# A cross-attention and quantized feed-forward kernel on one core: weight pieces turned as two-byte numbers, and the orders of all engines written anew

## The chip, the cores and the metric

The kernel runs on one core of a Trainium2 chip, in one launch. The metric is the device time of an execution in microseconds (us), as the median of the runs shown. TensorE multiplies and transposes into PSUM, VectorE (DVE), ScalarE (ACT) and GpSimd (POOL) work on tiles, and SyncE (SP) issues nearly all transfers.

## The reference

Eight items of 512 tokens with 512 features attend to 120 context rows with 16 heads, then pass a feed-forward layer whose weights are quantized to -1, 0 and 1 and whose activations are rounded to 8-bit steps:

```
x = x + attention(layernorm(x), ctx, ctx, mask, wq, bq, wk, bk, wv, bv, wo, bo)   # softmax over 120 keys
scale = 1 / clip(mean(|w|), 1e-5)
wq = clip(round(w * scale), -1, 1) / scale            # for w1 [2048, 512] and w2 [512, 2048]
xq = round(rmsnorm(x) * s) / s, s = 127 / max|row|
h = gelu(xq(layernorm(x)) @ wq1.T + b1)
x = x + xq(h) @ wq2.T + b2
```

## The kernel before, in words

The tokens are 32 tiles of 128 (four to an item). Attention goes by units n = 0 to 127, four to a tile (four heads each); normalize(n), exps(n) and turn_probs(n) belong to unit n. ffn_up(k, c) makes one of four chunks of the hidden row of tile k, ffn_down(k, half) the output. Each engine has one queue, written out by hand as a list of calls in order; four passes of a loop (a = 2 to 5) hold the middle, and lists without a loop the start and the end. An engine does its list strictly in order, and semaphores hold it where it needs another's result.

The weights w1 and w2 come in eight pieces of 128 x 2048 (piece 0 to 3 of w1, 4 to 7 of w2). Each is summed in absolute value on ScalarE or VectorE (sum_abs), TensorE adds up the sums (total_weights(0) after w1's four, total_weights(1) after w2's), and weight_scales gives w_inv. GpSimd rounds the piece in place (round_piece, two passes), TensorE turns it in 16 blocks of 128 x 128, four to a bank, alternately into ps_z and ps_y (turn_piece(j, quarters), j the place in TURN), and evac_piece copies each bank as fp8 into w1T or w2T, ps_z by ScalarE and ps_y by VectorE. A bank can't be written again before it is copied. The rounding adds MAGIC = 12582912 so that float32 itself rounds; the second pass clips, and the copy subtracts MAGIC:

```
gp.tensor_scalar(piece, piece, w_inv[:, m:m + 1], MAGIC, ALU.mult, ALU.add)
gp.tensor_scalar(piece, piece, MAGIC + 1.0, MAGIC - 1.0, ALU.min, ALU.max)
```

The attention weights are split into a high and a low part for products of three passes; for wo, ScalarE makes the high part (round_wo) and VectorE the low one (split_wo), from a stage that wq used before. The loads of pieces 5, 6 and 7 wait for buffers to come free. Where tile k's rounded rows q_x or q_h are wanted turned, SyncE issues a transposing transfer (turn_x, turn_h). keep_busy runs turns of the identity whose results nobody reads.

Of the kernel before, what the change touches and what calls it, by code (L numbers as in the profile page):

```python
# [28 lines left out]
def xattn_bitffn_kernel(nc, x, ctx_in, mask, wq, bq, wk, bk, wv, bv, wo, bo, w1, b1, w2, b2, out):  # L29
# [105 lines left out]
    with ExitStack() as stack:  # L135
# [17 lines left out]
        ident = sb("ident", [P, P])  # L153
        neg_half = sb("neg_half", [P, T])
# [164 lines left out]
        def _(sp):  # L319
# [62 lines left out]

            for t in range(T):
                sp.dma_start(xn[:, t], xt_v[0, t]).then_inc(s[f"first{t}_in"], 16)
# [8 lines left out]
            sp.wait_ge(s["turn_full"], YT_N[("x", 0, 3)] + 1)  # L393
            sp.dma_start(xn[:], x_v[1]).then_inc(s["x_in"], 16)
            sp.wait_ge(s["turn_full"], YT_N[("k", 0, 0)] + 1)
            sp.dma_start(ctx_s, ctx_in[1]).then_inc(s["ctx_in"], 16)
            sp.wait_ge(s["wq_split"], 1)
            sp.dma_start(stage.rearrange("p (k n) -> p k n", k=KD), wo.rearrange("(k p) n -> p k n", p=P)
                         ).then_inc(s["wo_in"], 16)
            sp.dma_start(bv_row[:], bv.rearrange("(a d) -> a d", a=1).to_broadcast([S2, D])).then_inc(s["bv_in"], 16)  # L400
            load_piece(4)
            for v, dst in ((bo, bo_row), (b1, b1_row), (b2, b2_row)):
                sp.dma_start(dst[:], v.rearrange("(a d) -> a d", a=1).to_broadcast([P, v.shape[0]])
                             ).then_inc(s["bias_in"], 16)

            load_residual(0)
            load_piece(6)
            load_piece(5)
            load_piece(7)
            load_x(2)  # L410
            load_residual(3)
            load_mask(1)
            load_residual(1)
            load_residual(2)
            turn_x(0)
            load_residual(5)
            load_ctx(2)
            turn_x(1)
            turn_x(2)
            load_residual(4)  # L420
            load_x(3)
            turn_h(0)
            turn_x(3)
            turn_h(1)
            store(0)
            load_mask(2)
            load_ctx(3)
            turn_h(2)
            store(1)
            load_residual(6)  # L430
            load_residual(7)
            turn_x(4)
            turn_h(3)

            for a in range(2, 6):
# [3 lines left out]
                store(4 * a - 5)  # L439
                turn_x(4 * a - 2)  # L440
                turn_h(4 * a - 4)
                load_x(a + 2)
                load_residual(4 * a + 1)
                turn_h(4 * a - 3)
                turn_x(4 * a - 1)
                store(4 * a - 4)
                load_mask(a + 1)
                load_ctx(a + 2)
                store(4 * a - 3)
                load_residual(4 * a + 3)  # L450
                load_residual(4 * a + 2)
                turn_x(4 * a)
                turn_h(4 * a - 2)
                turn_h(4 * a - 1)

            turn_x(21)
            turn_x(22)
            store(18)
            turn_h(20)
            load_residual(24)  # L460
            store(19)
            turn_x(23)
            turn_h(21)
            load_residual(25)
            load_mask(7)
            store(20)
            load_residual(26)
            turn_x(24)
            store(21)
            turn_h(22)  # L470
            turn_x(25)
            load_residual(27)
            turn_h(23)
            turn_x(26)
            store(22)
            turn_h(24)
            store(23)
            load_residual(28)
            turn_x(27)
            load_residual(29)  # L480
# [7 lines left out]
            load_residual(31)  # L488
            turn_h(27)
            turn_x(30)  # L490
            turn_h(28)
            turn_x(31)
            store(26)
            turn_h(29)
            turn_h(30)
            turn_last(0)
# [10 lines left out]
        def _(pe):  # L507
# [205 lines left out]
            def first_q(w, m, i):  # L713
# [3 lines left out]
                return last  # L717
# [1812 lines left out]
```

## Time and profile before

| | us |
|---|---|
| median of 3 runs | 658.78 |
| lowest, highest | 658.63, 660.31 |
| the profiled execution | 659.41 |
| its span in the profile | 657.6 |
| TensorE busy | 633.0 |
| VectorE busy | 576.8 |
| ScalarE busy | 528.3 |
| GpSimd busy | 517.9 |

The span runs from the first to the last instruction, the time of an execution includes what lies around it. Busy time counts instructions that overlap once. Matmuls are pipelined: their durations are longer than the distance from one to the next, which is read from the chain or from starts.

### The profile page before, as it was taken

To read this page: it belongs to the slowest core of one execution; us is meant where nothing else is said; L and a number is where in the kernel's file an instruction comes from. 1 tells how busy PE (TensorE), PEld (TensorE's weight loads), DVE (VectorE), ACT (ScalarE), POOL (GpSimd) and SP (SyncE) were. 2 spreads that over 40 slices of the span, in tenths; PEclk is the share of its full clock that TensorE was granted. 3 is DMA by queue.
4 is the path that set the end of the run, shared out by engine and by line. 5 is a ranking of instruction groups with operands and counts; after the bars stand their busy time and mean duration, and the time that the engine had idled before them with its cause. 6 is when DMAs were issued, how large, how long until landed. Compare 5 with 4: busy or idle time off the path is not lost.

```text
span 657.6 us, 14093 instructions
## 1 busy us (share of the span) xinstructions
PE 633.0 (96%) x4896; PEld 425.3 (65%) x4896; DVE 576.8 (88%) x1062; ACT 528.3 (80%) x1450; POOL 517.9 (79%) x653
## 2 busy tenths in 40 slices
PE   7969999999999999999999999999999999999996
PEld 6646786566666766666666666666766666666542
DVE  6578789999998989999899989999889898999994
ACT  2459678888888688888988788897989979999764
POOL 3276898679986898768877798768976788989875
PEclk9979999999999999999999999999999999999999
DMA  8991320225135324144344334243322323234336
GB/s 288 380 334 66 95 74 9 78 52 125 42 74 137 72 73 89 41 114 103 73 73 109 76 97 57 72 114 88 87 41 61 74 84 57 58 89 100 79 77 164
DMA packets 109285, 65.38 MB, mean 99 GB/s; under 512 B 90855, under 2 KB 90855, under 8 KB 108575
## 3 DMA queue, kind: packets, MB, share of 16 engines
q1 hardware_dynamic: 108159, 64.49, 37.1%
q8 instruction: 39, 0.64, 0.4%
q14 instruction: 31, 0.25, 0.1%
q10 hardware_dynamic: 1056, 0.00, 0.1%
HBM read 35.12 MB, written 8.39 MB: 66 GB/s over the span
## 4 chain that ended last, share of the span: by engine, by line
PE 60%; POOL 17%; DVE 7%; DMA 6%; ACT 5%; issue 4%; SPq 1%; POOLq 0%; DVEq 0%; ACTq 0%
PE ps_a L545 21%; PE ps_z L659 10%; PE ps_y L682 10%; PE ps_t L618 6%; PE ps_s L608 3%; POOL hid L2223 3%; POOL prob L2212 3%; PE ps_a L630 3%; POOL q_h L2228 3%; DMA x<-in_L_xattn_wo_dram 2%; PE ps_y L552 1%; PE ps_a L579 1%; POOL x L2207 1%; POOL x L2175 1%; PE ps_s L682 1%
## 5 line engine op out<-in xcount | busy, mean ns | idle before, releaser
L1110 ACT ACTIVATE prob<-ps_s,nmax 128x120 f32<-128x120 f32 x512 | 179.5, 381 | 17.3 <-PE ps_t L618 8.6
L2212 POOL TENSOR_TENSOR prob<-prob,pinv 128x480 f32<-128x480 f32 x128 | 128.9, 1011 | 60.9 <-DVE pinv L1545 60.3
L659 PE MATMUL ps_z<-w1T,q_xT 128*128 128x512 fp8e4 x476 | 122.6, 380 | 0.8 <-DVE hid L1586 0.5
L1110 ACT ACTIVATION_READ_ACCUMULATOR prob<-ps_s,nmax 128x1 f32 x512 | 115.7, 226 | 0.0
L682 PE MATMUL ps_y<-w2T,q_hT 128*128 128x512 fp8e4 x448 | 105.0, 379 | 1.3 <-DMA q_hT<-q_h 1.2
L1586 DVE SCALAR_TENSOR_TENSOR hid<-ps_z,y_deq,b_row 128x512 f32<-128x512 f32 x119 | 87.9, 739 | 11.2 <-PE ps_z L659 9.1
L1537 DVE COPY_PREDICATED_SCALAR ps_s<-hidden_key,masked_c 128x480 f32 x128 | 90.4, 706 | 0.7 <-PE ps_s L608 0.6
L1088 ACT COPY probT<-ps_t 120x512 f32<-120x512 f32 x128 | 76.8, 600 | 16.9 <-PE ps_t L618 14.5
L1540 DVE TENSOR_REDUCE nmax<-ps_s 128x4 f32<-128x480 f32 x128 | 84.2, 657 | 4.4
L618 PE MATMUL ps_t<-ident,prob 128*120 128x128 f32 x512 | 78.0, 275 | 2.2 <-ACT probT L1088 1.3
L618 PEld LDWEIGHTS ps_t<-ident,prob 128*120 128x120 f32 x512 | 60.2, 137 | 26.4 <-ACT probT L1088 5.2
L682 PEld LDWEIGHTS ps_y<-w2T,q_hT 128*128 128x128 bf16 x448 | 42.5, 98 | 50.3 <-issue 5.6
L659 PEld LDWEIGHTS ps_z<-w1T,q_xT 128*128 128x128 bf16 x476 | 42.8, 98 | 45.9 <-issue 8.7
L1594 DVE TENSOR_REDUCE hs<-hid 128x1 f32<-128x2048 f32 x31 | 70.4, 2271 | 0.9 <-ACT hid L1117 0.4
L2223 POOL TENSOR_SCALAR hid<-hid,hs 128x2048 f32<-128x2048 f32 x31 | 61.2, 1975 | 7.4 <-ACT q_h L1151 3.7
L1117 ACT ACTIVATE hid<-hid 128x2048 f32<-128x2048 f32 x31 | 59.3, 1914 | 3.9 <-DVE hid L1586 3.6
L2228 POOL TENSOR_SCALAR q_h<-hid 128x2048 bf16<-128x2048 f32 x28 | 53.8, 1920 | 2.5
L545 PE MATMUL ps_a<-wo_h,oT_h 128*128 128x512 f32 x128 | 54.2, 424 | 0.0
L1151 ACT ACTIVATE q_h<-hid 128x2048 bf16<-128x2048 f32 x28 | 54.2, 1934 | 0.0
L545 PE MATMUL ps_a<-wo_h,oT_l 128*128 128x512 f32 x128 | 50.4, 394 | 0.0
L545 PE MATMUL ps_a<-wo_l,oT_h 128*128 128x512 f32 x128 | 50.0, 391 | 0.0
L545 PE MATMUL ps_a<-xnT_h,wq_h 128*128 128x512 f32 x112 | 47.3, 422 | 0.0
(207 smaller groups left out, 1382.9 us busy)
## 6 DMA issues: line engine op xcount, KB each, us to landing
x<-in_x_dram SPq DMA_DIRECT2D x32, 256.0 KB, 3.0
out_dram<-x SPq DMA_DIRECT2D x32, 256.0 KB, 2.4
xn<-in_x_dram SPq DMA_DIRECT2D x7, 1024.0 KB, 6.2
hid<-in_L_ffn_w_dram SPq DMA_DIRECT2D x4, 1024.0 KB, 8.9
ctx_k<-in_ctx_dram SPq DMA_DIRECT2D x8, 240.0 KB, 3.1
ctx_k<-in_mask_Bx1xSxS_ik_dram SPq DMA_DIRECT2D x7, 240.0 KB, 3.1
xn<-in_x_dram SPq DMA_DIRECT2D x4, 256.0 KB, 4.8
x<-in_L_xattn_wq_dram SPq DMA_DIRECT2D x1, 1024.0 KB, 8.4
```

The lines of the kernel that those rows point to most:

```text
L545: last = nc.tensor.matmul(bank, w, m, start=(k == 0 and i == 0), stop=(k == KD - 1 and i == 2))
L618: last = nc.tensor.transpose(ps_t[0:S2, g * P:(g + 1) * P], prob[:, n % 3, g * S2:(g + 1) * S2], ident[:])
L659: last = nc.tensor.matmul(bank[:], q_xT[:, k % 3, i], w1T[:, i, c * CH:(c + 1) * CH], start=(i == 0), stop=(i == KD - 1))
L682: last = nc.tensor.matmul(y_bank(k)[:], turned_h(k)[:, f], w2T[:, f], start=(f == 0), stop=(f == KF - 1))
L1088: nc.scalar.copy(probT[0:S2, i], ps_t[0:S2, :].rearrange("p (g q) -> p g q", g=G)).then_inc(s["p_evac"], 1)
L1110: last = nc.scalar.activation(prob[:, n % 3, g * S2:(g + 1) * S2], ps_s[n % HG][:, g * S2:(g + 1) * S2], ACT.Exp, bias=nmax[:, n % 4, g:g ...
L1537: v.copy_predicated(sc, hidden_key[:, k // T % 2, k % T].unsqueeze(1).to_broadcast([P, G, S2]), masked_c[:].unsqueeze(2).to_broadcast([P, ...
L1540: v.tensor_reduce(out=nmax[:, n % 4], in_=sc, op=ALU.max, axis=AX_X, negate=True).then_inc(s["sc_max"], 1)
L1586: v.scalar_tensor_tensor(hidden(k)[:, c * CH:(c + 1) * CH], z_bank(FC * k + c)[:], y_deq[:, k % 8:k % 8 + 1], b1_row[:, c * CH:(c + 1) * C ...
L2212: gp.tensor_tensor(pr, pr, pinv[:, n % 4].unsqueeze(2).to_broadcast([P, HG, S2]), ALU.mult).then_inc(s["prob_ready"], 1)
L2223: gp.tensor_scalar(magic(k), hidden(k), hs[:, 5, t:t + 1], MAGIC, ALU.mult, ALU.add).then_inc(s["h_magic"], 1)
L2228: gp.tensor_scalar(rounded(k), hidden(k), 1.0, -MAGIC, ALU.mult, ALU.add).then_inc(s["qh_ready"], 1)
```

## The change

It has three parts. First, the second pass of round_piece takes MAGIC off, clips above at 1 and writes two-byte numbers (bfloat16) into the low half of the piece's own buffer; TensorE turns these with a two-byte identity into two-byte views of the banks; the copies clip below, ScalarE by the sign, VectorE by a maximum with -1. Second, first steps are moved: on SyncE the loads of wv, wo, bv, the biases and the second context, on TensorE the first project_ctx and 20 idle turns for 12, on VectorE hide, split_wq and weight_scales. Some waits go with them (wk_in is waited for in project_ctx, the bias columns in evac_q and add_bk). Third, the lists of all engines have a new order throughout, in the loop too, with the same calls in them.

```diff
+        ident_b = sb("ident_b", [P, P], BF16)
+        turned_z, turned_y = ps_z[:].bitcast(BF16)[:, 0:CH], ps_y[:].bitcast(BF16)[:, 0:CH]
+        def low_half(p):
+            return piece_buf[p].bitcast(BF16)[:, 0:F]
...
-            for p in range(4):
-                load_piece(p)
-            sp.dma_start(wv_s[:], wv.rearrange("(k p) n -> p k n", p=P)).then_inc(s["wv_in"], 16)
...
+            load_piece(0)
+            load_piece(2)
+            load_bv()
+            load_piece(1)
+            load_piece(3)
+            load_x(1)
+            load_wo()
+            load_wv()
+            load_next_ctx()
             load_piece(4)
...
             def turn_piece(j, quarters):
                 p = TURN[j]
+                if j == 0:
+                    pe.wait_ge(s["consts_pool"], 5)
...
-                        last = nc.tensor.transpose(bank[:, c * P:(c + 1) * P], piece_buf[p][:, col:col + P], ident[:])
+                        last = nc.tensor.transpose(bank[:, c * P:(c + 1) * P], low_half(p)[:, col:col + P], ident_b[:])
...
-                nc.scalar.activation(dst, src, ACT.Copy, bias=-MAGIC, saturate=False).then_inc(s["wT_act"], 1)
+                nc.scalar.activation(dst, src, ACT.Sign, saturate=False).then_inc(s["wT_act"], 1)
...
-                v.tensor_scalar(dst, src, -MAGIC, None, ALU.add, saturate=False).then_inc(s["wT_dve"], 1)
+                v.tensor_scalar(dst, src, -1.0, None, ALU.max, saturate=False).then_inc(s["wT_dve"], 1)
...
-                gp.tensor_scalar(piece, piece, MAGIC + 1.0, MAGIC - 1.0, ALU.min, ALU.max
+                gp.tensor_scalar(low_half(p), piece, -MAGIC, 1.0, ALU.add, ALU.min
                                  ).then_inc(s["w_ready_pool"], 1)
...
+            gp.tensor_copy(ident_b[:], ident[:]).then_inc(s["consts_pool"], 1)
...
             normalize(9)
+            round_piece(4)
+            ln1_factors(2, 0, 4, 9)
+            normalize(10)
             round_x(0)
```

GpSimd, behind its copy of wq's high part: L2263 and L2266 are the two passes of round_piece, L2157 to L2162 the factors of item 1's layernorm, L2168 its application to a tile, L2212 normalize. Before:

```order
L2263 TENSOR_SCALAR hid<-hid,w_inv 128x2048
L2266 TENSOR_SCALAR hid<-hid 128x2048
L2263 TENSOR_SCALAR hid<-hid,w_inv 128x2048
L2266 TENSOR_SCALAR hid<-hid 128x2048
L2157 TENSOR_SCALAR ln<-mv 128x4
L2160 TENSOR_TENSOR ln<-ln,neg_half 128x4
L2162 TENSOR_SCALAR ln<-mv 128x4
L2263 TENSOR_SCALAR raw_wk_h<-raw_wk_h,w_inv 128x2048
L2266 TENSOR_SCALAR raw_wk_h<-raw_wk_h 128x2048
L2212 TENSOR_TENSOR prob<-prob,pinv 128x480 x2
L2168 TENSOR_SCALAR xn<-xn,ln 128x512 x4
```

The same place in the change, where the lines are L2305, L2308, L2199 to L2204, L2210 and L2254:

```order
L2305 TENSOR_SCALAR hid<-hid,w_inv 128x2048
L2308 TENSOR_SCALAR hid<-hid 128x2048
L2199 TENSOR_SCALAR ln<-mv 128x4
L2202 TENSOR_TENSOR ln<-ln,neg_half 128x4
L2204 TENSOR_SCALAR ln<-mv 128x4
L2210 TENSOR_SCALAR xn<-xn,ln 128x512 x2
L2305 TENSOR_SCALAR hid<-hid,w_inv 128x2048
L2308 TENSOR_SCALAR hid<-hid 128x2048
L2305 TENSOR_SCALAR raw_wk_h<-raw_wk_h,w_inv 128x2048
L2308 TENSOR_SCALAR raw_wk_h<-raw_wk_h 128x2048
L2254 TENSOR_TENSOR prob<-prob,pinv 128x480 x3
L2210 TENSOR_SCALAR xn<-xn,ln 128x512 x2
```

The factors and two tiles of x moved ahead of pieces 1 and 2.

GpSimd again, from piece 6 or 7 to the first round_x (L2180 and L2185; q_hT is piece 4's buffer). Before:

```order
L2263 TENSOR_SCALAR hid<-hid,w_inv 128x2048
L2266 TENSOR_SCALAR hid<-hid 128x2048
L2212 TENSOR_TENSOR prob<-prob,pinv 128x480
L2180 TENSOR_SCALAR yw<-yw,yq 128x512
L2185 TENSOR_SCALAR q_x<-yw 128x512
L2212 TENSOR_TENSOR prob<-prob,pinv 128x480
L2263 TENSOR_SCALAR q_hT<-q_hT,w_inv 128x2048
L2266 TENSOR_SCALAR q_hT<-q_hT 128x2048
```

In the change, where round_x is L2222 and L2227:

```order
L2305 TENSOR_SCALAR hid<-hid,w_inv 128x2048
L2308 TENSOR_SCALAR hid<-hid 128x2048
L2254 TENSOR_TENSOR prob<-prob,pinv 128x480
L2305 TENSOR_SCALAR q_hT<-q_hT,w_inv 128x2048
L2308 TENSOR_SCALAR q_hT<-q_hT 128x2048
L2199 TENSOR_SCALAR ln<-mv 128x4
L2202 TENSOR_TENSOR ln<-ln,neg_half 128x4
L2204 TENSOR_SCALAR ln<-mv 128x4
L2254 TENSOR_TENSOR prob<-prob,pinv 128x480
L2222 TENSOR_SCALAR yw<-yw,yq 128x512
L2227 TENSOR_SCALAR q_x<-yw 128x512
```

The first round_x moved behind piece 4 and the factors of item 2.

TensorE at the end of a pass of the loop: L682 is ffn_down (x16 is both halves), L659 ffn_up, L618 turn_probs, L630 attend, L608 scores. Before:

```order
L618 MATMUL ps_t<-ident,prob 120x128 x4
L659 MATMUL ps_z<-w1T,q_xT 128x512 x4
L630 MATMUL ps_a<-probT,v_s 32x128 x16
L682 MATMUL ps_y<-w2T,q_hT 128x512 x16
L659 MATMUL ps_z<-w1T,q_xT 128x512 x4
L608 MATMUL ps_s<-keyT,qT 128x120 x16
```

In the change, in the same order of names L640, L681, L652, L704, L681, L630:

```order
L704 MATMUL ps_y<-w2T,q_hT 128x512 x8
L681 MATMUL ps_z<-w1T,q_xT 128x512 x4
L640 MATMUL ps_t<-ident,prob 120x128 x4
L652 MATMUL ps_a<-probT,v_s 32x128 x16
L704 MATMUL ps_y<-w2T,q_hT 128x512 x8
L681 MATMUL ps_z<-w1T,q_xT 128x512 x4
L630 MATMUL ps_s<-keyT,qT 128x120 x16
```

The first half of ffn_down moved ahead of one ffn_up, a turn_probs and attend.

## Rows read from the trace of the kernel before

**Rows 1.** The page: busy time by engine, the transfer rate by slice, one costly group.
```profile
PE 633.0 (96%) x4896; PEld 425.3 (65%) x4896; DVE 576.8 (88%) x1062; ACT 528.3 (80%) x1450; POOL 517.9 (79%) x653
...
GB/s 288 380 334 66 95 74 9 78 52 125 42 74 137 72 73 89 41 114 103 73 73 109 76 97 57 72 114 88 87 41 61 74 84 57 58 89 100 79 77 164
...
L2228 POOL TENSOR_SCALAR q_h<-hid 128x2048 bf16<-128x2048 f32 x28 | 53.8, 1920 | 2.5
```

**Rows 2.** Stretches: busy us of PE, PEld, DVE, ACT, POOL; clock, DMA share, GB/s.
```profile
33.00:50.00 17.00, 11.45 (x48) 7.19 (x48) 12.17 (x19) 8.53 (x30) 13.37 (x10) 0.80 0.91 320
...
62.00:98.00 36.00, 35.64 (x311) 28.38 (x312) 28.82 (x63) 26.49 (x104) 29.17 (x25) 1.00 0.26 77
98.00:160.00 62.00, 60.25 (x504) 39.51 (x503) 59.30 (x111) 54.00 (x154) 49.10 (x61) 1.00 0.23 58
160.00:550.00 390.00, 387.14 (x3044) 263.83 (x3036) 352.61 (x656) 330.51 (x923) 317.80 (x411) 1.00 0.34 81
```

**Rows 3.** The chain that ended last: start, length, what; x counts loads too.
```profile
22.54 13.77 DMA x<-in_L_xattn_wo_dram
...
40.80 5.26 PE ps_a L579 x8
...
62.96 3.43 PE ps_a L579 x8
...
82.57 0.44 PE ps_z L705 x4
...
83.88 1.05 PE ps_a L630 x32
...
98.03 0.86 PE ps_z L659 x4
...
252.60 3.56 PE ps_y L682 x16
...
639.12 4.24 DMA q_hT<-xn
```

**Rows 4.** Timeline of TensorE; the idle time before and its releaser stand in brackets.
```profile
38.86 1.09 PE L705 MATMUL ps_z<-ident,hid 128*128 128x128 f32 x4 [4.77 <-ACT w1T L1169]
...
61.91 0.36 PE L691 MATMUL ps_z<-w_abs,q_xT 128*128 128x4 f32 x2
...
97.86 1.03 PE L659 MATMUL ps_z<-w1T,q_xT 128*128 128x512 fp8e4 x4
```

**Rows 5.** VectorE's copies of turned pieces, by form, up to 140 us: busy us, mean ns.
```profile
L1672 DVE TENSOR_SCALAR w1T<-ps_y 128x512 fp8e4<-128x512 f32 x8 | 5.5, 688 | 5.6 <-PE ps_y L705 5.6
```

**Rows 6.** VectorE by form in the last 28 us.
```profile
L1632 DVE TENSOR_SCALAR probT<-qT 128x1024 bf16<-128x1024 f32 x1 | 0.7, 694 | 0.0
```

**Rows 7.** Timeline of GpSimd.
```profile
28.99 1.98 POOL L2263 TENSOR_SCALAR hid<-hid,w_inv 128x2048 f32<-128x2048 f32 x1 [15.33 <-DVE w_deq L1644]
...
37.37 1.02 POOL L2160 TENSOR_TENSOR ln<-ln,neg_half 128x4 f32<-128x4 f32 x1
...
49.66 3.02 POOL L2168 TENSOR_SCALAR xn<-xn,ln 128x512 f32<-128x512 f32 x4
...
65.68 2.88 POOL L2212 TENSOR_TENSOR prob<-prob,pinv 128x480 f32<-128x480 f32 x3 [5.83 <-DVE pinv L1545]
...
79.43 0.99 POOL L2212 TENSOR_TENSOR prob<-prob,pinv 128x480 f32<-128x480 f32 x1 [1.80 <-DVE pinv L1545]
...
85.68 0.69 POOL L2180 TENSOR_SCALAR yw<-yw,yq 128x512 f32<-128x512 f32 x1
```

**Rows 8.** Timeline of VectorE: the first statistics of item 1.
```profile
32.04 0.69 DVE L1523 BATCH_NORM_STATS2 bn<-xn 128x6 f32<-128x512 f32 x1 [3.16 <-DMA xn<-in_x_dram]
```

**Rows 9.** DMA issues, us to landing: turn_x, then turn_h.
```profile
q_xT<-q_x SPq DMA_TRANSPOSE x32, 2.4
q_hT<-q_h SPq DMA_TRANSPOSE x29, 4.3
```

**Rows 10.** Timeline of SyncE: the issue of ffn_down(6)'s turned rows, and the next.
```profile
246.17 12.82 SPq L352 DMA_TRANSPOSE q_hT<-q_h  x2
```

More of the change, by code:

```diff
@@ L938, in _ @@
             ffn_up(21, 1)
+            attend(23)
             ffn_down(19, 1)
-            attend(23)
+            ffn_up(21, 2)
             scores(25)
-            ffn_up(21, 2)
             turn_probs(97)
@@ L1054, in _ @@
             ffn_up(30, 2)
+            ffn_up(30, 3)
             ffn_down(27, 0)
-            ffn_up(30, 3)
             ffn_down(27, 1)
-            ffn_down(28, 0)
             ffn_up(31, 0)
@@ L1062, in _ @@
             ffn_up(31, 3)
+            ffn_down(28, 0)
             ffn_down(28, 1)
@@ L1809, in _ @@
+            invert_sums(19)
             softmax_max(20)
-            evac_up(1, 1)
-            invert_sums(19)
-            oT_low(3)
+            softmax_max(21)
             xT_low(2, 2)
-            softmax_max(21)
+            softmax_max(22)
             evac_up(1, 2)
-            softmax_max(22)
+            residual(3)
             invert_sums(20)
-            residual(3)
             softmax_max(23)
+            ln2_stats(3)
             evac_up(1, 3)
+            ln2_scales(3)
+            add_bv(2)
@@ L1907, in _ @@
                 residual(4 * a - 1)
+                evac_up(4 * a - 2, 0)
+                invert_sums(16 * a + 5)
                 softmax_max(16 * a + 7)
@@ L1964, in _ @@
             oT_low(22)
+            invert_sums(94)
             softmax_max(96)
+            invert_sums(95)
             xT_low(7, 0)
-            invert_sums(95)
+            evac_up(20, 3)
             softmax_max(97)
+            softmax_max(98)
+            residual(22)
+            evac_up(21, 0)
             invert_sums(96)
-            evac_up(20, 3)
-            residual(22)
+            ln2_stats(22)
             xT_low(7, 1)
-            softmax_max(98)
-            ln2_stats(22)
+            invert_sums(97)
@@ L2012, in _ @@
+            add_bk(7)
+            evac_up(23, 0)
             softmax_max(107)
-            invert_sums(104)
-            add_bk(7)
-            ln2_stats(24)
-            evac_up(23, 0)
             h_scale(22)
-            invert_sums(105)
             invert_sums(106)
-            ln2_scales(24)
-            invert_sums(107)
             evac_up(23, 1)
-            evac_down(21)
             oT_low(25)
             softmax_max(108)
+            softmax_max(109)
             evac_up(23, 2)
-            softmax_max(109)
@@ L2028, in _ @@
-            invert_sums(108)
             softmax_max(110)
             softmax_max(111)
+            evac_up(23, 3)
+            evac_down(21)
+            invert_sums(107)
+            hide(7, mask_in)
+            invert_sums(108)
+            residual(25)
+            ln2_stats(25)
             invert_sums(109)
-            evac_up(23, 3)
-            residual(25)
-            hide(7, mask_in)
-            ln2_stats(25)
+            ln2_scales(25)
             evac_up(24, 0)
-            ln2_scales(25)
+            invert_sums(110)
```

958 lines of the change are left out of this document (489 added, 469 removed).

## Prediction

> **What bounds the kernel now.** I read the page's shares first: TensorE is busy 633.0 of 657.6 us, VectorE 88%, ScalarE 80%, GpSimd 79% [rows 1]. An average over stages says little, so the stretches come next: from 160 to 550 us TensorE is busy 387.14 of 390 us, so no order of the same work can win more than 2.9 us there. Between 33 and 50 us it is busy 11.45 of 17 at a mean clock of 0.80, and from there to 98 us it is nearly full [rows 2]. The gain, if any, lies ahead of 98 us: in the 5.55 us that TensorE idles at 33 to 50, and in the work it does there.
>
> The chain says what holds it: the load of wo, issued at 22.54, lands 13.77 us later at 36.31 [rows 3]; ScalarE rounds wo ahead of its first copy of a weight piece, and TensorE waits 4.77 us for that copy's bank, until 38.86 [rows 4]. In the stretch behind this wait the granted clock is lower: eight passes over wv take 5.26 us at 40.80, and the like take 3.43 at 62.96 [rows 3]. The marks that I follow are the second total of the weights on TensorE (61.91) and the first ffn_up (97.86) [rows 4]: 35.95 us apart, TensorE nearly gapless between them [rows 2].
>
> **The cheaper transposes.** Four turns of two-pass float32 follow in 0.44 us, 110 ns each [rows 3]. A two-byte turn streams 128 columns in one pass. The nearest row is the 512-column product of one-pass operands, four in 0.86 us, 215 ns each [rows 3]; a quarter is 54. So 56 ns less each, 128 turns: 7.2 us of TensorE work. Bounds: 54 ns, and no gain (110). I take 54, since the passes over wv (429 ns for 512 columns, 3.43/8) show the same factor of two for float32 against one pass. On the path lie those between the two marks, 64 turns (pieces 4 to 7): 3.6 us. The other 64 lie where TensorE waits, and the wait hides them.
> The Trainium skill, TensorE: Matmul & The Clock Gate, section Back-to-back issue gap, speaks against a quarter: it gives about 81 ns for a sustained pair of a weight load and a 128-column product. By it, the 64 turns would save 1.9 us, TensorE's leg below would be 33.6 and pass GpSimd's, and the time would be 1.1 us above mine. No row of before shows such a pair in two-byte form.
>
> **The copies out of PSUM.** VectorE's now reads two-byte numbers and takes a maximum; it took 688 ns from float32 to fp8 [rows 5]. Not shown by any row. Above: 0.69 us, nothing won. Below: the two-byte output of 1024 elements from SBUF took 694 ns [rows 6], so 512 might take 0.35, 16 copies 5.4 us of VectorE, which would take away the loss of 1.8 below: 649.3. I take 0.69: source is PSUM and output one byte, as in the present row. ScalarE's Sign for Copy I leave at nothing: the order of the changed kernel has no table load among them. It has one pair of table loads more in the body, in ScalarE, which idles a fifth of the span [rows 1].
> The Trainium skill, DVE: opcode table, section Perf-mode slots, says that a one-source operation with an fp8 stream does not reach the modes that ask for two-byte source and destination. The sum by it is the sum above.
> GpSimd's second pass over a piece now writes two bytes: 1920 ns for such an output [rows 1] against 1.98 us for the first pass [rows 7]; a piece stays at 3.97 with the hand-over. The copy of the identity, 128 by 128, lies before GpSimd's factors, which wait for x anyway.
>
> **The moved loads.** wv goes behind x of item 1 and wo; bv goes ahead of them, and the second context behind. At 380 GB/s [rows 1] the megabyte is 2.8 us, bv's 0.24 MB 0.6. Piece 3 lands 0.6 later, so w_inv, for which GpSimd waited 15.3 us until 28.99 [rows 7], comes at 29.6. x lands at 32.04 - 2.8 + 0.6 = 29.8 [rows 8]; wo at 36.3 - 2.8 = 33.5 (bv's and the context's bytes cancel). wv lands last, about where wo did (36.3), still ahead of its use. SyncE then waits for the turned keys before piece 4 and the biases, until about 28.5. Their users come after 50 us, so nothing. On TensorE the first project_ctx goes ahead of first_q and eight more idle products stand ahead of x; both lie in front of w_inv, which is set by the loads: nothing, cover 1.5 to 2 us; without it as much would be paid.
>
> **To the first mark.** GpSimd's queue is now: piece 0, factors of item 1, two tiles of x, pieces 1 and 2, three normalizations, two tiles, piece 3, one normalization. Pieces 4 x 3.97 = 15.9; factors 1.7 (1.02 for the power, the rest two small ones and hand-overs); four tiles 3.0; four normalizations at 0.96 = 3.8 (2.88 for three) [rows 7]: 24.4 with nothing between. VectorE has its statistics of x ready at 29.8 + 4.1 = 33.9 (four of 0.69 [rows 8] with an aggregation each, and add_bk), 0.3 after piece 0. So 29.6 + 24.4 + 0.3 = 54.3, and with the turn and the total behind it 54.9. Before, the mark was 61.91. The other bound is ScalarE: from wo's landing to the mark were 25.6 us, which with wo at 33.5 gives 59.1 if no wait in it shortens. But ScalarE is busy 8.53 of 17 us at 33 to 50 [rows 2]; 3.3 of the idle lie ahead of wo, so some 5 of the 25.6 were waits for TensorE's turns, and its leg could end at 54. So I choose near the shorter: 55.9, 6.0 earlier.
>
> **To the first ffn_up.** GpSimd again: from the mark to piece 5's start 6.6 us as before (61.91 to 68.56) [rows 4, 7]; four pieces 15.9, normalizations 7 to 10 3.8, factors 1.7, round_x 1.4 (0.69 and about as much) [rows 7], the turn of q_x 2.4 [rows 9], 0.7 for the wait of normalization 8: 32.5, so 88.4. TensorE's own leg is 35.95 - 3.6 - 0.4 (one turn of probabilities moved behind) = 31.9, less than 32.5: GpSimd sets it by 0.6, since round_x(0) now stands behind piece 4 and the factors. 97.86 becomes 88.4: 9.5 earlier.
>
> **Behind it.** At 98 to 160 VectorE is busy 59.3 of 62 [rows 2]. Between evac_up(0, 0) and (0, 1) it now has ln2_scales(1) and a piece's copy where one softmax_max stood. It can keep the gain only as far as it was early itself. The loss is between nothing and the 3.5 us won between the marks; I take half, 1.8. The body (2.9 us of idle in 390) I take as unchanged. So is the end: TensorE there waits for the turn of q_h, 4.24 us from 639.12 [rows 3], behind GpSimd's round_h, and the square that now goes ahead of round_h(29) on ScalarE fits the wait.
> Sum: 9.5 - 1.8 = 7.7 us. The profiled execution took 659.41 (span 657.6 and 1.8 around it) and becomes 651.7; the median of the runs is 658.78, 0.6 less: **651.1**.
>
> **Rivals.** *A, the same path with another end* (0.58): 647 to 654.
> *B, GpSimd's queue holds the first ffn_up* (0.13). Normalization 8 started at 79.43, after a wait [rows 7], 17.5 after the mark, because its reciprocal stood behind residual(0). If it stays there: 55.9 + 17.5 = 73.4, then 1.0, pieces 6, 7, 4 11.9, two normalizations 1.9, factors 1.7, round_x 1.4, turn 2.4: 93.7, only 4.2 early; less 1.8 that is 656.4. For it: three things that wait for piece 4 now. Against: the reciprocal is ahead of residual(0) in the new order.
> *C, VectorE gives back all that was won between the marks* (0.08): 6.0 early, 652.8; or the turns cost what they did (0.02): TensorE's leg is 35.5, 3.0 over GpSimd's, 654.1.
> *D, the body and the end also gain* (0.06): 2.9 us of idle and half of the 4.24: up to 5 us, 646.
> *E, within 0.3%* (0.08): B, and the ScalarE bound of 59.1 too. The mark is then 2.8 early and the rest gives back: about 657.
> *F, slower* (0.05): ffn_down(4a - 2, 0) has moved ahead of an ffn_up, a turn and attend, 0.86 + 0.44 + 1.05 = 2.35 us earlier [rows 3]. Its q_hT was issued at 246.17 [rows 10] and lands 4.3 later [rows 9], at 250.5, used at 252.60 [rows 3]: 2.1 us of room. round_h stands one normalization (0.96) earlier, so 0.7 is left. If round_h comes 3.1 us late, because the reductions ahead of it on VectorE do, each of four passes of the loop loses 2.4, 9.6 in all, against 7.7 won: 660.7. It decides from about 2.7 us late on.
>
> **The numbers.** 651.1, range 646 to 656.5: D's lower end is left out in part, and E and F above; the lost share is about 0.17. 0.3% is 2 us, about what this kernel's runs can tell. Faster (A to D) 0.87, same (E) 0.08, slower (F) 0.05.
>
> **What would show it.** Right: turns four in 0.22 us; VectorE's piece copy at 0.69; TensorE's wait for the first copy's bank under 3 us; second total near 56; first ffn_up near 88, with TensorE waiting for q_xT; TensorE still idle under 4 us from 160 to 550. Wrong: turns at 0.32 or more for four, piece 3 ready after 57, DVE at full share from 85 on while TensorE idles, waits for q_hT in the loop.

## The result and the profile after

The changed kernel took 695.62 us (median of 4 runs, 694.57 to 695.95), the kernel before 659.07 beside it (658.63 to 660.31): a ratio of 1.056, 95% interval 1.054 to 1.058. I had forecast 651.1, faster. The profiled execution took 695.95, its span is 694.1.

First the shares on the page of after, which answer to [rows 1]: GpSimd has 40.1 us more work, no other engine over 7.3 more, and TensorE's share fell from 96% to 92%.

```profile
PE 640.3 (92%) x4904; PEld 430.4 (62%) x4904; DVE 579.8 (84%) x1062; ACT 533.0 (77%) x1452; POOL 558.0 (80%) x654
```

The stretches of after, with the columns of [rows 2], say where: the body at 160 to 550 us is as full as before, and nearly everything is lost ahead of it. There GpSimd is the busiest engine in every stretch, and from 50 us on TensorE's granted clock, which was 1.00 before, is down too.

```profile
33.00:50.00 17.00, 8.53 (x62) 5.41 (x60) 8.80 (x14) 7.18 (x21) 16.56 (x8) 0.80 0.47 158
50.00:62.00 12.00, 2.45 (x20) 1.84 (x21) 4.12 (x6) 4.34 (x12) 11.91 (x4) 0.56 0.75 272
62.00:98.00 36.00, 26.89 (x212) 18.61 (x210) 22.64 (x44) 21.12 (x69) 28.55 (x16) 0.83 0.17 56
98.00:160.00 62.00, 50.24 (x424) 37.02 (x423) 44.85 (x81) 38.45 (x124) 55.05 (x44) 0.88 0.08 22
160.00:550.00 390.00, 387.09 (x3050) 261.71 (x3049) 355.12 (x663) 335.94 (x926) 319.92 (x408) 1.00 0.36 83
```

TensorE's timeline of after names what it waits for (in brackets at a line's end), one of GpSimd's second passes (L2308) in each line with a wait but the last. The second total, 61.91 in [rows 4], now stands at 78.24, and the first ffn_up, 97.86 before, at 133.73.

```profile
40.15 0.58 PE L729 MATMUL ps_z<-ident_b,hid 128*128 128x128 bf16 x4 [6.82 <-POOL hid L2308]
...
61.62 0.61 PE L729 MATMUL ps_z<-ident_b,raw_wk_h 128*128 128x128 bf16 x4 [6.70 <-POOL raw_wk_h L2308]
...
78.24 0.42 PE L713 MATMUL ps_z<-w_abs,q_xT 128*128 128x4 f32 x2
...
116.83 0.61 PE L729 MATMUL ps_z<-ident_b,hid 128*128 128x128 bf16 x4 [6.50 <-POOL hid L2308]
...
133.73 1.02 PE L681 MATMUL ps_z<-w1T,q_xT 128*128 128x512 fp8e4 x4 [1.02 <-DMA q_xT<-q_x]
```

The eight waits for that line come to 36.4 us, in the list of waits of after by buffer:

```profile
PE ps_z L729 <- POOL hid L2308: 18.0, 4, 6.8
PE ps_z L729 <- POOL raw_wk_h L2308: 6.7, 1, 6.7
PE ps_z L729 <- POOL x L2308: 4.3, 1, 4.3
PE ps_z L729 <- POOL raw_wv_h L2308: 4.2, 1, 4.2
PE ps_z L729 <- POOL q_hT L2308: 3.2, 1, 3.2
```

GpSimd's groups by form give the reason (last columns: busy us, mean ns of one). The second pass takes 7.09 us, and the first pass over the same elements (L2305) 1.98, as in [rows 7]. The pass that writes two-byte q_h with (mult, add), on which I had rested my price [rows 1], is still at 1.91.

```profile
L2270 POOL TENSOR_SCALAR q_h<-hid 128x2048 bf16<-128x2048 f32 x28 | 53.5, 1909 | 2.5
...
L2308 POOL TENSOR_SCALAR hid<-hid 128x2048 bf16<-128x2048 f32 x4 | 28.4, 7092 | 0.3
...
L2305 POOL TENSOR_SCALAR hid<-hid,w_inv 128x2048 f32<-128x2048 f32 x4 | 7.9, 1979 | 17.4 <-DVE w_deq L1678 17.4
```

Three things set the new pass apart from the quick ones: its pair of operations (add, min), its place (the low half of its own source), and a clip with a two-byte output. The experiments begin there.

### The profile page after: what moved, and what is told of

The parts are those of the page before. It is cut to its first block, busy times and chain, and to the rows that moved or that the text cites. A ratio compares the mean times of both kernels' runs of the same rounds, so it can differ in the third digit from the quotient of the medians.

```text
span 694.1 us, 14117 instructions
## 1 busy us (share of the span) xinstructions
PE 640.3 (92%) x4904; PEld 430.4 (62%) x4904; DVE 579.8 (84%) x1062; ACT 533.0 (77%) x1452; POOL 558.0 (80%) x654
## 4 chain that ended last, share of the span: by engine, by line
PE 52%; POOL 29%; DVE 7%; issue 5%; DMA 3%; ACT 3%; SPq 0%; POOLq 0%; DVEq 0%; ACTq 0%
PE ps_a L567 16%; PE ps_z L681 9%; PE ps_y L704 9%; PE ps_t L640 5%; POOL prob L2254 5%; POOL hid L2308 4%; POOL hid L2265 3%; PE ps_s L630 3%; PE ps_a L652 3%; POOL q_h L2270 2%; DMA q_hT<-q_h 2%; PE ps_y L574 1%; DVE ps_s L1571 1%; POOL x L2249 1%; ACT prob L1141 1%
## 5 line engine op out<-in xcount | busy, mean ns | idle before, releaser
L2254 POOL TENSOR_TENSOR prob<-prob,pinv 128x480 f32<-128x480 f32 x128 | 129.2, 1013 | 37.0 <-DVE pinv L1579 36.8
L681 PE MATMUL ps_z<-w1T,q_xT 128*128 128x512 fp8e4 x476 | 123.5, 382 | 2.0 <-DMA q_xT<-q_x 1.5
L1141 ACT ACTIVATION_READ_ACCUMULATOR prob<-ps_s,nmax 128x1 f32 x512 | 111.8, 218 | 0.0
L704 PE MATMUL ps_y<-w2T,q_hT 128*128 128x512 fp8e4 x448 | 105.6, 379 | 1.3 <-DMA q_hT<-q_h 1.3
L640 PE MATMUL ps_t<-ident,prob 128*120 128x128 f32 x512 | 80.2, 280 | 2.3 <-POOL prob L2254 2.0
L640 PEld LDWEIGHTS ps_t<-ident,prob 128*120 128x120 f32 x512 | 60.6, 140 | 24.0 <-issue 6.8
L704 PEld LDWEIGHTS ps_y<-w2T,q_hT 128*128 128x128 bf16 x448 | 42.3, 98 | 50.8 <-issue 6.1
L681 PEld LDWEIGHTS ps_z<-w1T,q_xT 128*128 128x128 bf16 x476 | 43.0, 98 | 48.5 <-issue 9.0
L567 PE MATMUL ps_a<-wo_h,oT_h 128*128 128x512 f32 x128 | 56.3, 440 | 0.0
```

What stands on the lines that cost most here:

```text
L567: last = nc.tensor.matmul(bank, w, m, start=(k == 0 and i == 0), stop=(k == KD - 1 and i == 2))
L640: last = nc.tensor.transpose(ps_t[0:S2, g * P:(g + 1) * P], prob[:, n % 3, g * S2:(g + 1) * S2], ident[:])
L681: last = nc.tensor.matmul(bank[:], q_xT[:, k % 3, i], w1T[:, i, c * CH:(c + 1) * CH], start=(i == 0), stop=(i == KD - 1))
L704: last = nc.tensor.matmul(y_bank(k)[:], turned_h(k)[:, f], w2T[:, f], start=(f == 0), stop=(f == KF - 1))
L1141: last = nc.scalar.activation(prob[:, n % 3, g * S2:(g + 1) * S2], ps_s[n % HG][:, g * S2:(g + 1) * S2], ACT.Exp, bias=nmax[:, n % 4, g:g ...
L2254: gp.tensor_tensor(pr, pr, pinv[:, n % 4].unsqueeze(2).to_broadcast([P, HG, S2]), ALU.mult).then_inc(s["prob_ready"], 1)
```

## The experiments

Eleven kernels ran, in three groups (e0 to e4, e5 to e8, e9 to e11), with the kernel before beside each group at medians of 659.01, 658.12 and 658.26 us. Ratios are to those runs.

The places in time come from one profiled execution of each kernel, and they move between executions. Ahead of the first passes over wv, the kernels e4, e6, e7, e8 and e11 have the same code, and yet TensorE reached the passes over wv between 36.49 us (e6, where the granted clock stayed at 1.00 from 28 us on) and 39.47 us (e7, where it was 0.50 from 30 to 34). Differences of a us or two between places in two kernels are to be read with that in mind.

**The pass by itself (e0).** New kernel; its core, with one line for each pair, type and place:

```python
gp.tensor_scalar(wide[:], d[:], -MAGIC, 1.0, ALU.add, ALU.min)             # and six other pairs
gp.tensor_scalar(narrow[:], d[:], -MAGIC, 1.0, ALU.add, ALU.min)           # the same seven, two-byte output
gp.tensor_scalar(p0[:].bitcast(BF16)[:, 0:F], p0[:], -MAGIC, 1.0, ALU.add, ALU.min)
```

> This kernel leaves the whole computation out: one weight piece (128 x 2048, scaled and with the magic number added) is loaded, GpSimd runs tensor_scalar passes over it one after the other with nothing else on the chip, then VectorE does; the output is filled from one of them. In the changed kernel the pass (add, min) from float32 into the two-byte low half of its own buffer takes 7.08 us; the pass (mult, add) from float32 to two bytes in another buffer takes 1.91 us, and (min, max) from float32 to float32 in place took 1.9 us. Three theories. T1, the pair: (add, min) is slow for any output, the float32 one too: 7.1 us in wide, narrow and in place, and (mult, add) and (min, max) take 1.9 us in all. T2, the place: out-of-place passes take 1.9 us whatever the pair and the type; all passes into the low half of their own source take 7.1 us. T3, the type with a clip: float32 output 1.9 us for every pair; two-byte output 1.9 us for (mult, add) and 7.1 us for every pair with a min or a max. T4, contention in the full kernel (VectorE shares the port): everything takes 1.9 us here, since VectorE stands still. I hold T1 for the likeliest (0.5), T3 next (0.3), T2 0.15, T4 0.05. Half the columns in (add, min) should take half the time by T1.

GpSimd's groups, the slow ones first. Into another buffer in float32, by line: 85 (add, min), 89 (min, add), 93 (add, add), 101 (max, add), 77 (mult, add), 97 (add, mult), 81 (min, max). In place in float32: 141 (add, min). Into the low half of the source: 133 (add, min), 135 (mult, add). Line 145 is (add, min) over half the columns.

```profile
L89 POOL TENSOR_SCALAR wide<-d 128x2048 f32<-128x2048 f32 x1 | 7.1, 7091 | 0.1
L93 POOL TENSOR_SCALAR wide<-d 128x2048 f32<-128x2048 f32 x1 | 7.1, 7091 | 0.1
...
L141 POOL TENSOR_SCALAR p<-p 128x2048 f32<-128x2048 f32 x1 | 7.1, 7091 | 0.1
...
L133 POOL TENSOR_SCALAR p<-p 128x2048 bf16<-128x2048 f32 x1 | 7.1, 7089 | 0.1
...
L101 POOL TENSOR_SCALAR wide<-d 128x2048 f32<-128x2048 f32 x1 | 7.1, 7084 | 0.1
...
L85 POOL TENSOR_SCALAR wide<-d 128x2048 f32<-128x2048 f32 x1 | 7.1, 7079 | 0.1
...
L145 POOL TENSOR_SCALAR narrow<-d 128x1024 bf16<-128x1024 f32 x1 | 3.6, 3626 | 0.1
...
L77 POOL TENSOR_SCALAR wide<-d 128x2048 f32<-128x2048 f32 x1 | 1.9, 1902 | 13.4 <-DVE p L62 13.4
...
L97 POOL TENSOR_SCALAR wide<-d 128x2048 f32<-128x2048 f32 x1 | 1.9, 1900 | 0.1
...
L135 POOL TENSOR_SCALAR p<-p 128x2048 bf16<-128x2048 f32 x1 | 1.9, 1900 | 0.1
...
L81 POOL TENSOR_SCALAR wide<-d 128x2048 f32<-128x2048 f32 x1 | 1.9, 1895 | 0.1
```

T1 holds, the others fall. (mult, add), (min, max) and (add, mult) take 1.90 us; (add, min), (min, add), (add, add) and (max, add) take 7.08, in float32 as in two bytes, in place as elsewhere, with VectorE standing still. Half the columns take half. VectorE's passes over the same data took 1.23 us for each of the three pairs tried, (add, min) too: of the two engines, only GpSimd told them apart.

**The change in two halves (e1, e2).** e1 is after with the weight path of before; e2 is before with the weight path of after. Their difference to the parent, e2's core:

```diff
-                gp.tensor_scalar(piece, piece, MAGIC + 1.0, MAGIC - 1.0, ALU.min, ALU.max
+                gp.tensor_scalar(low_half(p), piece, -MAGIC, 1.0, ALU.add, ALU.min
...
-                        last = nc.tensor.transpose(bank[:, c * P:(c + 1) * P], piece_buf[p][:, col:col + P], ident[:])
+                        last = nc.tensor.transpose(bank[:, c * P:(c + 1) * P], low_half(p)[:, col:col + P], ident_b[:])
```

> The changed kernel with the old weight path: second pass (min, max) in float32 in place, turns of float32, copies that subtract the magic number; all new orders and moved loads stay. If the slow second pass of GpSimd alone made the change slower (8 x 5.2 = 41 us more of GpSimd): about 654.7 us, my forecast of 651.1 with the 3.6 us of the 64 turns given back, range 650 to 659; the second total near 56 and the first ffn_up near 92. Rival, the new orders themselves cost: 680 us or more, and then the pass only filled time in which GpSimd waited anyway.

> The kernel before with the new weight path alone: the identity's cast to two bytes, the second pass (add, min) into the low half, two-byte turns, Sign and max in the copies; all orders as before. If the slow pass is the cause: each of eight pieces takes 5.2 us more on GpSimd, which is what the second total (four pieces) and the first ffn_up (all eight) wait for; second total at 61.9 + 20.8 less GpSimd's slack ahead of it (some 5), first ffn_up near 97.9 + 41.6 - 8 = 131, the time 659 + 33 = 692, range 685 to 700. Rival, the orders are the cause: under 665 us here.

e1: 658.82 us, ratio 1.001 (0.9994 to 1.0027). e2: 693.81 us, ratio 1.053 (1.050 to 1.057). The weight path makes the whole loss. The orders have no part in it, and are worth nothing that can be measured either, where I had 654.7. In e1's timeline the second total is at 61.14 and the first ffn_up at 96.41.

**One pair for the other (e4).** After, with

```diff
-                gp.tensor_scalar(low_half(p), piece, -MAGIC, 1.0, ALU.add, ALU.min
+                gp.tensor_scalar(low_half(p), piece, 1.0, -MAGIC, ALU.mult, ALU.add
...
-                v.tensor_scalar(dst, src, -1.0, None, ALU.max, saturate=False).then_inc(s["wT_dve"], 1)
+                v.tensor_scalar(dst, src, -1.0, 1.0, ALU.max, ALU.min, saturate=False).then_inc(s["wT_dve"], 1)
```

> The changed kernel with the pair of the second pass alone changed: (mult 1.0, add -magic) into the same low half, no clip on GpSimd; Sign clips both sides on ScalarE, and VectorE's copy takes (max -1, min 1) in one instruction. By T1 (the pair) and T3 (a clip with a two-byte output) the pass takes 1.9 us and this is the kernel that I forecast: 651.1 us, range 647 to 656; second total near 56, first ffn_up near 88. By T2 (a narrow output over its own source) the pass stays at 7.1 us and the time at 695.

657.58 us, ratio 0.9975 (0.9960 to 0.9989); the second pass takes 1.90 us. So 38.0 of the 44.5 us between forecast and result come from the pair alone. The kernel that I had in mind is this one, and it missed 651.1 too, by 6.5. Its timeline of TensorE shows more than one cause:

```profile
37.79 0.38 PE L729 MATMUL ps_z<-ident_b,hid 128*128 128x128 bf16 x4 [1.12 <-ACT w1T L1200]
38.01 0.39 PE L729 MATMUL ps_y<-ident_b,hid 128*128 128x128 bf16 x4
38.23 3.65 PE L601 MATMUL ps_a<-wv_s,ctxT 128*120 128x512 f32 x8
...
47.85 0.61 PE L729 MATMUL ps_z<-ident_b,raw_wk_h 128*128 128x128 bf16 x4 [2.70 <-POOL raw_wk_h L2308]
...
50.62 5.05 PE L601 MATMUL ps_a<-wk_s,ctxT 128*120 128x512 f32 x8
...
61.21 0.36 PE L713 MATMUL ps_z<-w_abs,q_xT 128*128 128x4 f32 x2
...
95.24 1.02 PE L681 MATMUL ps_z<-w1T,q_xT 128*128 128x512 fp8e4 x4 [0.84 <-DMA q_xT<-q_x]
```

Four turns follow in 0.22 us (38.01 to 38.23), 55 ns each, as forecast. But TensorE waits 2.70 us for piece 2, and eight passes over wk then take 5.05 us where the like over wv took 3.65: the granted clock is 0.50 from 48 to 52 us in the table of stretches, the lower of its two levels (1.2 against 2.4 GHz), right behind that wait. And piece 2 is late because of its first pass, on GpSimd's timeline:

```profile
41.79 4.02 POOL L2305 TENSOR_SCALAR raw_wk_h<-raw_wk_h,w_inv 128x2048 f32<-128x2048 f32 x1
```

It takes 4.02 us there and 1.97 for the other pieces. On VectorE, the subtraction for wo_l (two SBUF sources) began at 41.68 and took 2.28. In the kernel before, GpSimd's timeline has a pass of that kind too, but it is a normalization (0.99 otherwise), and piece 2 is past:

```profile
42.80 2.91 POOL L2212 TENSOR_TENSOR prob<-prob,pinv 128x480 f32<-128x480 f32 x1
```

**Idle products (e6), the subtraction elsewhere (e7), both (e8).** All from e4. e6 has 24 idle products into the free bank ahead of the wait for piece 2; e7 moves VectorE's split_wo from ahead of invert_sums(0) to behind evac_piece(1, 3); e8 does that and has 6 idle products. e6's core:

```diff
+                if j == 2 and quarters[0] == 0:
+                    wait(pe, "wT_act", 2 * j)
+                    for _ in range(24):
+                        nc.tensor.transpose(ps_z[:, 0:P], ident[:], ident[:])
                 wait(pe, *ready(p))
```

> The changed kernel with the fast pair, and 24 idle products of TensorE (2.6 us at 110 ns) in the 2.70 us in which it waits for piece 2 on GpSimd; behind that wait the granted clock is 0.5 from 48 to 53 and eight passes over wk take 5.05 us where they took 3.65 at the full clock. Theory C (the clock took the forecast gain): the clock stays at full speed, the passes take 3.6, the second total comes near 58.5 in place of 61.2, and the time falls by 1.5 to 2.7 us to 655 to 656. Rival G (GpSimd and VectorE set the total anyway): the clock is restored but piece 3 (rounded at 56.2) and the copies hold the total; at most 0.7 us, 657.

> The changed kernel with the fast pair, and VectorE's subtraction for wo_l moved behind its copies of piece 1. It lay at 41.68 for 2.28 us, at the same time as GpSimd's first pass over piece 2, which took 4.02 us there and 1.97 for every other piece. Theory L (the two hold each other up): the first pass over piece 2 takes 1.97, piece 2 is ready 2 us earlier (45.7), the collision moves to the normalizations at 46 to 49 (one takes 3 us), TensorE waits under 1 us for piece 2, and the time falls by 0.5 to 2 us. Rival (the long pass comes from data or DMA and not from the subtraction): it stays at 4 us. The load of piece 5 starts 2.5 us later; should the sum over piece 5 hold the second total, the time stays at 657.6.

> The changed kernel with the fast pair, the subtraction for wo_l moved as in the run ahead, and 6 idle products in what is left of the wait for piece 2. If clock and collision are the two things that held the second total at 61.2: near 57.5, and the time near 654.5 (653 to 656). If TensorE's chain behind 50 us (waits for the copies of pieces 2 and 3 and for the maxima) holds it: no better than the better of the two runs ahead.

e6: 656.15 us, ratio 0.9973 (0.9952 to 0.9993). The timeline of TensorE in e6:

```profile
49.43 3.65 PE L601 MATMUL ps_a<-wk_s,ctxT 128*120 128x512 f32 x8
...
58.62 0.36 PE L713 MATMUL ps_z<-w_abs,q_xT 128*128 128x4 f32 x2
...
59.95 5.07 PE L601 MATMUL ps_a<-wv_s,ctxT 128*120 128x512 f32 x8
...
94.31 1.02 PE L681 MATMUL ps_z<-w1T,q_xT 128*128 128x512 fp8e4 x4 [0.82 <-DMA q_xT<-q_x]
```

Theory C holds for the second total: the passes over wk are back at 3.65, and the total comes 2.6 us earlier than in e4. Piece 2 was turned 0.4 earlier, so 2.2 is the clock's. A second execution bears it out: e11 below has the same idle products, reached the passes over wv at 38.04, as e4 did (38.23), and had the total at 58.80.

Of the 2.6, 0.9 is left at the first ffn_up. Most of the rest went to the clock again: it fell right behind the total (0.50 from 60 to 62 us), and the next passes over wv took 5.07 us where they took 3.60 in e4. The profiled span is 2.5 shorter than e4's (653.9 against 656.4). A gain in time is not shown: the medians differ by 1.4, but the kernel before was 0.9 faster beside e6 than beside e4, and the ratios are 0.9973 and 0.9975.

e7: 657.37 us (0.9968 to 1.0002). Theory L holds for the mechanism: on GpSimd's timeline the first pass over piece 2 is back at 1.97, and two normalizations, 0.99 each otherwise, now take 3.98.

```profile
41.73 1.97 POOL L2305 TENSOR_SCALAR raw_wk_h<-raw_wk_h,w_inv 128x2048 f32<-128x2048 f32 x1
...
45.65 3.98 POOL L2254 TENSOR_TENSOR prob<-prob,pinv 128x480 f32<-128x480 f32 x2
```

The time did not move. The second total is at 60.86: TensorE waited 1.33 us for ScalarE's copy of piece 2 instead, and the clock fell again (wk in 4.88). This execution had reached the passes over wv 1.2 us later than e4's, so the stretch from there to the total did get shorter, 21.4 us for 23.0. e8: 657.72 us (0.9967 to 1.0000), which misses my 654.5. The collision had moved to the normalizations, TensorE waited 2.18 us for one of them, and the passes over wk took 5.74. So e8 took one wait away and met another behind it; of these three kernels none had both the collision and the low clock away.

**Side by side (e9).** GpSimd passes beside VectorE operations of the same size, in new kernel code like that of e0.

> This kernel leaves the whole computation out. GpSimd does three passes over 128 x 2048 float32, and VectorE beside it two operations of the same size, in six stretches: GpSimd's pair is (mult, add), which took 1.90 us alone, then (add, min), 7.09 us alone; VectorE's operation is a subtraction of two SBUF tensors (2.28 us beside GpSimd in the full kernel), a one-source (mult, add) (1.23 us alone), and a sum along the row. In the full kernel GpSimd's first pass over piece 2 took 4.02 us beside the subtraction for wo_l and 1.97 when that was moved. Theory L, they exclude each other, and whichever comes second waits for the whole of the other: beside the subtraction a fast pass takes up to 4.2 us or the subtraction up to 4.2, and beside a slow pass the subtraction takes up to 9 us while the pass stays at 7.1; beside the sum along the row nothing changes. Rival: they share the way to SBUF, and both take longer by the same share, the sum along the row too. For the one-source operation I expect the same as for the subtraction if its 1.23 us (half a cycle per element less than the sum's) come from a second way in.

The timeline: first VectorE's subtraction (L63, L65) beside (mult, add) on GpSimd, then its sum along the row (L77), then the subtraction beside (add, min), and last VectorE's one-source (mult, add) (L93) beside (add, min).

```profile
9.41 2.28 DVE L63 TENSOR_TENSOR vwide<-d,e 128x2048 f32<-128x2048 f32 x1
9.58 3.87 POOL L109 TENSOR_SCALAR wide<-d 128x2048 f32<-128x2048 f32 x1 [9.14 <-DVE tick L62]
11.72 3.86 DVE L65 TENSOR_TENSOR vwide<-d,e 128x2048 f32<-128x2048 f32 x1
...
27.43 2.28 DVE L77 TENSOR_REDUCE red<-d 128x1 f32<-128x2048 f32 x1
27.67 1.90 POOL L123 TENSOR_SCALAR wide<-d 128x2048 f32<-128x2048 f32 x1 [0.40 <-DVE tick L76]
...
33.69 2.28 DVE L84 TENSOR_TENSOR vwide<-d,e 128x2048 f32<-128x2048 f32 x1
33.92 8.98 POOL L130 TENSOR_SCALAR wide<-d 128x2048 f32<-128x2048 f32 x1 [0.40 <-DVE tick L83]
36.00 6.46 DVE L86 TENSOR_TENSOR vwide<-d,e 128x2048 f32<-128x2048 f32 x1
...
57.62 7.91 POOL L137 TENSOR_SCALAR wide<-d 128x2048 f32<-128x2048 f32 x1 [0.40 <-DVE tick L90]
58.63 7.98 DVE L93 TENSOR_SCALAR vwide<-d 128x2048 f32<-128x2048 f32 x1
```

Beside a quick pass they exclude each other. The first to start keeps its own duration, 2.28; the second stretches by about what is left of the first, 1.90 to 3.87 and 2.28 to 3.86. The sum along the row disturbs nothing. VectorE's one-source (mult, add), 1.23 us alone, takes part too: a quick pass beside it took 2.73, and behind a slow pass it took 7.98 itself and ended 1.1 us after that pass (66.61 and 65.53), so it waited for all of it.

The subtraction behind a slow pass did not. It took 6.46 where I had expected up to 9, and it ended at 42.46, 0.44 us before the pass (42.90). The same shows in the changed kernel: wo_l's subtraction took 4.11 us there, from 47.88, and ended 0.45 us before the slow pass beside it (45.35, 7.09 long). So a slow pass keeps the subtraction out for a part of its time only; what decides on that part, no run shows.

The Trainium skill, SBUF — State Buffer, section Who interferes with whom, states this: a VectorE instruction with two SBUF inputs, or in a two-port mode, and a GpSimd instruction that reads SBUF hold a shared pair of ports exclusively, and the later one blocks. The runs agree for quick passes and for the one-source operation. For the subtraction behind a slow pass they don't: a block for what was left of the pass would have made it 6.90 + 2.28 = 9.2 us long, an estimate from these lines, and it took 6.46.

**GpSimd with one pass (e10), piece 5 first (e11).** e10 is e1 without GpSimd's second pass; ScalarE's copy takes the sign of the number less MAGIC, VectorE's subtracts MAGIC and clips below, and the clip above is left out there. e11 is e6 with round_piece(5) ahead of normalize(4).

```diff
-                                 ).then_inc(s["w_round_pool"], 1)
-                pool.wait_ge(s["w_round_pool"], i + 1)
-                gp.tensor_scalar(piece, piece, MAGIC + 1.0, MAGIC - 1.0, ALU.min, ALU.max
                                  ).then_inc(s["w_ready_pool"], 1)
...
-                v.tensor_scalar(dst, src, -MAGIC, None, ALU.add, saturate=False).then_inc(s["wT_dve"], 1)
+                v.tensor_scalar(dst, src, -MAGIC, -1.0, ALU.add, ALU.max, saturate=False).then_inc(s["wT_dve"], 1)
```

> The new orders with float32 turns and no second pass on GpSimd at all: the turned numbers still hold the magic number; ScalarE's copy takes Sign(x - magic), VectorE's takes (add -magic, max -1), which leaves out the clip above (numbers over 1 stay, so half of the weights are not those of the reference). It takes 8 x 1.9 = 15.2 us from GpSimd against the run with the new orders alone (658.8) and leaves TensorE's turns at 110 ns. If GpSimd's queue sets the second total and the first ffn_up, as my prediction had it: piece 2 is ready near 42, TensorE does not wait for it, the clock stays up, second total near 57, first ffn_up near 92.5 (TensorE's own leg of 35.5), time 654 to 656. If TensorE's own chain and the copies set them: over 657.5, and the 5.2 us of the slow pass would have been hidden too, which the 695 speaks against.

> The run with the idle products (656.2), and on GpSimd piece 5 ahead of normalizations 4, 5 and 6. GpSimd stood idle 7.1 us between 58 and 67, waiting for reciprocals, while w_inv of w2 was there from 59.7 on; piece 5 was begun at 67.94, 9.3 us behind the second total, where I had forecast 6.6. If GpSimd sets the first ffn_up: TensorE's wait of 0.82 us for q_xT goes, the first ffn_up comes at 93.5 or earlier in place of 94.31, and the time falls by 0.5 to 1 us to 655.4. It can win no more, since TensorE idles only 1.6 us between the second total and the first ffn_up. Rival: normalization 4 comes 1.7 us late, TensorE waits for the turned probabilities at 66, and the time rises to 657.

e10: 658.38 us, ratio 0.9992 (0.9976 to 1.0008): nothing, though GpSimd has 15 us less. In the profiled execution the first total came 1.1 us later than in e4 (30.50 for 29.43) and the clock was low until 37 us, so TensorE reached the passes over wv 3.0 later (41.24 for 38.23). The stretch from there to the second total is what can be compared: 20.2 us here, 23.3 in e1, 23.0 in e4. So GpSimd's queue, with the clock that fell behind the wait for it, held e1 and e4 by 3 us in this stretch. In e10 TensorE is busy at the full clock for all but 2.5 us, and what it waits for is mostly the copies of the turned pieces:

```profile
50.99 0.63 PE L730 MATMUL ps_z<-ident,raw_wk_h 128*128 128x128 f32 x4 [0.71 <-ACT w1T L1203]
...
59.91 0.63 PE L730 MATMUL ps_z<-ident,raw_wv_h 128*128 128x128 f32 x4 [0.99 <-ACT w1T L1203]
```

Neither of the two cases that I had set out is what happened: GpSimd can hold the mark only down to the 20 us that TensorE and the copies need. What a shorter queue of GpSimd is worth this execution can't say, since it came 3.0 us late for another reason: it turned piece 2 at 48.52, and GpSimd had that piece ready at 47.9 even in e1. The second total is at 61.46, no earlier than e1's.

e11: 657.67 us (0.9974 to 1.0003). TensorE still waits 0.81 us for q_xT, at 94.09 where I had 93.5 or earlier, and 1.09 for a normalization at 65.03, as the rival said. It tells the theories apart no further.

**The fourth corner (e5).** Before, with the two-byte path of e4.

> The kernel before with the two-byte weight path in its fast form (second pass mult, add into the low half; Sign and max/min in the copies), all orders as before: the fourth corner beside before (659.0), the new orders alone (658.8) and both (657.6). If orders and path add up: 659.0 - 1.2 = 657.8, range 656.5 to 659. If the path is worth more on its own, because TensorE is gapless from 62 to 98 in the old order and the 64 turns there save 3.6 us: 655.5, and then the new orders cost 2 us. If the path is worth nothing without the orders: 659.

656.84 us, ratio 0.9981 (0.9963 to 0.9999); second total at 60.55, first ffn_up at 94.90. With the quick pair the path is worth 1.3 us in the old order and 1.2 in the new (657.58 for 658.82), so the two parts add up, as the first of my three cases had it. Of the 3.5 us that 64 turns save between the second total and the first ffn_up, 1.2 show there (34.03 us in e4, 35.27 in e1), 1.4 went into waits that e4 has and e1 has not (0.84, 0.30 and 0.22), and 0.9 I can't place.

## Why the prediction was wrong

**The step that failed** is the price of GpSimd's second pass: "1920 ns for such an output", "a piece stays at 3.97 with the hand-over". The output was such, the pair was not. The row that I took it from was (mult, add), the row before (min, max), and no row of before had (add, min). I bounded VectorE's new copy from both sides and took this one from one row. It cost 5.2 us a piece (7.09 for 1.9), 41.5 for eight. The sum needs 38: 17.0 of it are there at the second total (78.24 against e4's 61.21, four pieces at 5.2 are 20.8, less slack), 38.5 at the first ffn_up (133.73 against 95.24). No rival of mine had it, and the slower one, F, named another place. With the right pair the sign would have been right by a little, and the size not.

**The turns**: right, 55 ns. The Trainium skill, TensorE: Matmul & The Clock Gate, section Back-to-back issue gap, has 81 ns for sustained pairs of a weight load and a 128-column product; the runs here show 55 ns, in streams of eight turns (37.79 to 38.23 in e4).

**The copies**: right. VectorE's took 690 ns from two-byte PSUM, with one operation or two; ScalarE's Sign 0.60 us.

**The moved loads**: nearly. GpSimd's first piece began at 30.81 in after (30.63 in e4), where I had 29.6. The wait for the first copy's bank fell from 4.77 to 1.12 us in e4, as forecast.

**The first mark**: too early by 5.3 us even with the right pair (61.21 for 55.9). I followed two legs, GpSimd's and ScalarE's, and worked out none for TensorE. With GpSimd nearly out of the way it needs 20.2 us from the passes over wv to the mark (e10, turns of 110 ns). From 38.2, that is 58.4, less at most 2.6 for 48 cheaper turns, 55.8, an estimate. So 55.9 asked for a TensorE that never waits for GpSimd. In e4 it does wait, 2.70 us for piece 2: wo_l's subtraction had put 2.05 us on that piece (e7, e9), and w_inv was 1.0 late. And behind that wait the clock was low, worth 2.2 (e6). The two together are 4.9 of the 5.3. Neither collision nor clock was in my sum, though [rows 3] showed what a wait does to the passes behind it.

**From there to the first ffn_up**: 34.0 us in e4 where I had 32.5, and TensorE did end in a wait for q_xT (0.84), behind GpSimd. Piece 5 began 7.6 behind the mark, not 6.6.

**Behind it**: I took off 1.8 for VectorE. In e4 nothing was lost: round_h's first pass, at 126.2 before, began 4.1 earlier, and the last, at 637.8, 2.6 earlier, as much as at the first ffn_up. Its median is 1.4 under that of before, so about 1.2 is lost behind 635 us, where TensorE waits 3.3 for the turn of q_x of the last tile. I called the end unchanged; no run tried it apart, so the cause of these 1.2 us stays open.

Together for e4: 6.8 late at the first ffn_up, less 1.8 not lost, and 1.2 at the end: 6.2 of the 6.5.

## What to carry to other kernels

A price belongs to an instruction with its operations, not to its shape and type: take it from a row with the same pair, or bound it from both sides, on GpSimd above all. Where pieces arrive one by one, work out TensorE's own leg too, with the clock that its waits will leave it, before calling another engine the bound. Ahead of a move, list what the other of VectorE and GpSimd will do at that time: a subtraction of two SBUF tensors puts nearly its full time on a GpSimd pass that starts just behind it. And before a place in one profile is compared with the same place in another, look at the granted clock ahead of both.

## What the runs showed of the hardware

- GpSimd's two-operation pass over 128 x 2048 float32: 1.90 us for (mult, add), (min, max), (add, mult); 7.08 for (add, min), (min, add), (add, add), (max, add), in every output type and place tried; VectorE 1.23 us for each of three pairs, (mult, add), (min, max) and (add, min).
- VectorE's subtraction and a quick GpSimd pass wait for each other: 1.90 became 3.87, 2.28 became 3.86. Behind a slow pass the subtraction took 6.46 and ended 0.44 us before the pass; a one-source operation took 7.98 and waited for the whole pass. The sum along the row (2.28) disturbed nothing.
- The clock at half speed behind a wait of 2.70 us made eight passes over wk 5.05 us long, where 24 idle products (2.79 us) in that wait kept them at 3.65, in two executions (e6, e11).
- Where the code ahead was the same, the clock fell or held from one execution to the next, and TensorE reached the same place at 36.49 to 39.47 us.
